# Products with B kept in their PSUM bank and scanned from there, in the two scan attentions of a four-layer adaLN network, with the order of all engines' steps laid out anew

## The chip, the cores and the metric

One Trainium2 chip, one of its cores. The time is the device time in microseconds of one launch of the whole program; the profile is of one further execution of the same program on the same core.

## The reference, cut to what matters

Four layers, each an attention-like block and a feed-forward block with adaLN modulation, on x of 4 x 512 x 128 values (2,048 rows of 128). Two of the attention-like blocks hold a recurrence along the sequence of 2,048 rows. The text calls them by the kernel's names: L2A is the retention block with index 2 ("the second" of the change's words), L3A the selective state-space block with index 3 ("the third").

```
# L2A (retention), per head of 8 channels: a decaying state of outer products of k and v
scores[i, j] = (q_i . k_j) * decay ** (i - j)   for j <= i
out          = group_norm(scores @ v) @ WO
# L3A (state space), 128 channels D, 16 states N
dt = softplus(x @ Wdt + bdt);  A = -exp(A_log)
h[t] = exp(dt[t] * A[:, n]) * h[t-1] + dt[t] * x[t] * B[t, n]      # for each n of 16
y[t] = sum over n of C[t, n] * h[t][:, n];  out = (y * silu(z)) @ Wout
```

The kernel lays channels on the 128 partitions and rows of the sequence along the free dimension. So L3A's recurrence is, for each n, one scan over 512 columns of h = A*h + B*dx, with dx = dt*x, and L2A's is, for each of 8 columns n of v, one scan of s = decay*s + k*v.

## The kernel before, in words

**Strands.** The 2,048 rows are cut into four chunks of W = 512. Each chunk c (0 to 3) runs through all eight blocks (L0A, L0F, L1A, L1F, L2A, L2F, L3A, L3F) as a strand; a fifth strand is the preparation. For each engine and block there is a generator (`l3a_tensor`, `l3a_vector`, ...) whose `yield`s cut it into steps. A string of letters, ORDER (4,524 letters before), says whose step is laid down next: a to e are TensorE's steps of strands 0 to 4, f to j ScalarE's, k to o VectorE's, p to t GpSimd's, u to y SyncE's. So each engine's instruction queue is a fixed merge of its strands, and an instruction that waits holds up all behind it, those of other strands too.

**Banks.** PSUM's eight banks are given out in the same order: `banks.take(s, q, name, step)` takes the bank whose last user lets go first, makes TensorE wait for that, and notes `step` as what will free it.

**L3A.** For each n of 16 TensorE spreads row n of B and of C over all partitions into a bank each (`B%d`, `C%d`, L1928 and L1931: a one-hot column times a bf16 split of B and C in three parts). ScalarE makes A = exp(dt*A_n) into one of four buffers AH (L1976). For even n VectorE multiplies the bank by dx into a buffer of the three in BH (L2027) and scans it in place (L2035). For odd n ScalarE copies the bank into that buffer (L1985), GpSimd multiplies it there by dx (L2059), and VectorE scans it (L2035). Then VectorE multiplies the C bank by the scanned state into A's buffer (L2039), ScalarE keeps the state's last column for the next chunk (`carry3`, L1989), GpSimd adds A's buffers of each two n (`sum`, L2065), and TensorE adds the sum to bank Y with an identity matmul (L1939). A scan of chunk c > 0 begins with chunk c-1's last column.

**L2A.** TensorE makes column n of v in all places (L1592), for even n VectorE multiplies the bank by k into a buffer of four, KV (L1663), for odd n ScalarE copies the bank (L1623) and GpSimd multiplies it by k (L1715). VectorE scans each in place with a decay that is one value to a partition (L1671), ScalarE keeps the last column (L1627), GpSimd multiplies by q (L1721), and TensorE sums over the key's eight channels into bank R (L1597).

**Around them.** While strands 0 and 1 are in L3A (about 625 to 770 us) the others' L0F, L2A and L2F run beside them; while 2 and 3 are in L3A (about 970 to 1,112 us) L2F of strand 3 and L3F of strands 0 and 1 do, whose weights come by indirect DMA from GpSimd's queue (L2459) and whose rows go out and back through SyncE's and GpSimd's (L2511, L2517, L2462, L2442).

## Time and profile before

| | us |
|---|---|
| median of 3 runs | 1228.77 |
| lowest, highest | 1224.02, 1233.12 |
| the profiled execution | 1225.84 |
| its span in the trace | 1223.8 |

In the profile a row of engine busy time counts instructions from start to end; two that follow each other at once overlap a little. "Idle before, releaser" is the time that the engine stood still ahead of the instruction and what ended it. PE is TensorE's matmul side, PEld its weight loads, DVE VectorE, ACT ScalarE, POOL GpSimd. PEclk is the granted TensorE clock as a share of the full one. The chain is the work that ended last, followed back from the last instruction.

### The profile page before, as it was taken

What the parts mean: (1) busy time and instruction counts of PE and PEld (TensorE: products, weight loads), DVE (VectorE), ACT (ScalarE), POOL (GpSimd) and SP (SyncE); (2) the same over time, 40 slices, a digit from 0 to 9 for tenths busy, and PEclk for the clock granted to TensorE, in tenths of its full rate; (3) what the DMA queues carried; (4) which work ended last, traced back from release to release, by engine and by line L of the source; (5) the groups of instructions that cost most, each with busy time, mean ns of one, the idle gap of its engine ahead of it and who ended that gap; (6) DMA issues with size and microseconds to landing.
All of it is one profiled execution on the core that took longest, in us unless ns stands there. A gap on an engine that the chain in (4) does not pass through costs nothing.

```text
span 1223.8 us, 18281 instructions
## 1 busy us (share of the span) xinstructions
PE 1082.9 (88%) x6855; PEld 654.4 (53%) x6855; DVE 872.7 (71%) x2050; ACT 685.5 (56%) x1155; POOL 493.8 (40%) x475
## 2 busy tenths in 40 slices
PE   7999999899999899999999867779899987659978
PEld 5766544344444354456444313464568676338868
DVE  4745547567666768788799899675686989966446
ACT  4477566686745586655676724562525786544221
POOL 2014122212213520184246456525455465686363
PEclk9999999999999789999999868769799998869989
DMA  8103000000000000000000000000514043147583
GB/s 257 57 9 138 1 1 0 1 1 2 1 1 18 1 2 1 20 1 1 18 1 1 0 0 1 1 3 33 172 52 166 33 164 112 33 168 232 209 291 92
DMA packets 36071, 70.14 MB, mean 57 GB/s; under 512 B 3088, under 2 KB 26128, under 8 KB 35472
## 3 DMA queue, kind: packets, MB, share of 16 engines
q0 software_dynamic: 9680, 45.88, 10.6%
q1 hardware_dynamic: 26304, 23.10, 6.0%
q8 instruction: 54, 0.88, 0.3%
q14 instruction: 33, 0.27, 0.1%
HBM read 59.34 MB, written 9.63 MB: 56 GB/s over the span
## 4 chain that ended last, share of the span: by engine, by line
PE 60%; DVE 14%; POOL 8%; ACT 8%; issue 6%; DMA 2%; another core or an unknown queue 1%; DVEq 0%; SPq 0%; POOLq 0%; ACTq 0%
PE ps L899 9%; PE ps L2177 5%; PE ps L1477 5%; PE ps L2185 3%; DVE own L2035 2%; PE ps L861 2%; PE ps L673 2%; PE ps L1276 2%; PE ps L1751 1%; PE ps L659 1%; POOL own L2059 1%; POOL own L1721 1%; PE ps L1455 1%; PE ps L1754 1%
## 5 line engine op out<-in xcount | busy, mean ns | idle before, releaser
L899 PE MATMUL ps<-own,g_f 128*128 128x512 f32 x320 | 147.8, 602 | 0.1
L899 PEld LDWEIGHTS ps<-own,g_f 128*128 128x128 f32 x320 | 59.2, 191 | 67.2 <-issue 61.0
L1226 POOL TENSOR_TENSOR own<-own 128x512 f32<-128x512 f32 x32 | 40.1, 1254 | 131.1 <-PE ps L899 95.5
L2035 DVE TENSOR_TENSOR_SCAN own<-own,carry 128x512 f32<-128x512 f32 x48 | 77.7, 1618 | 15.5 <-POOL own L2059 13.6
L2059 POOL TENSOR_TENSOR own<-own 128x512 f32<-128x512 f32 x32 | 50.7, 1585 | 53.2 <-ACT own L1985 53.0
L1939 PE MATMUL ps<-own,g_c 128*128 128x512 f32 x64 | 44.5, 784 | 30.5 <-POOL own L2065 30.4
L1976 ACT ACTIVATE own<-own,Acol 128x512 f32<-128x512 f32 x64 | 45.2, 714 | 40.1 <-PE ps L1939 38.9
L1895 POOL TENSOR_TENSOR own<-own 128x512 f32<-128x512 f32 x32 | 44.5, 1392 | 55.7 <-DVE own L1869 35.9
L1477 PE MATMUL ps<-g_l,own 128*128 128x512 f32 x128 | 59.5, 611 | 7.7 <-issue 7.3
L531 ACT ACTIVATE own<-xs,sm 128x128 f32<-128x128 f32 x128 | 52.5, 483 | 24.0 <-POOL sm L523 24.0
L2399 DVE TENSOR_TENSOR own<-ps,own 128x512 f32<-128x512 f32 x53 | 36.1, 682 | 41.4 <-PE ps L2177 13.3
L2257 ACT ACTIVATE own<-ps 128x512 f32<-128x512 f32 x53 | 31.2, 596 | 60.1 <-PE ps L2177 49.4
L514 POOL TENSOR_SCALAR sm<-sm 128x4 f32<-128x4 f32 x32 | 9.5, 299 | 135.6 <-DVE sm L506 134.8
L1721 POOL TENSOR_TENSOR own<-own 128x512 f32<-128x512 f32 x32 | 45.0, 1408 | 37.5 <-ACT carry L1627 37.5
L1396 DVE SCALAR_TENSOR_TENSOR own<-ps,own 128x512 f32<-128x512 f32 x64 | 43.0, 683 | 21.6 <-ACT own L1365 21.4
L1362 ACT ACTIVATE own<-ps 128x512 f32<-128x512 f32 x64 | 37.5, 587 | 31.1 <-PE ps L1276 30.4
L1108 DVE TENSOR_TENSOR own<-own 128x512 f32<-128x512 f32 x32 | 27.9, 871 | 36.9 <-PE ps L899 35.1
L2177 PE MATMUL ps<-own,early 128*128 128x128 f32 x384 | 50.2, 281 | 1.4 <-issue 1.4
L2177 PEld LDWEIGHTS ps<-own,early 128*128 128x128 f32 x384 | 48.2, 197 | 4.9 <-issue 4.4
L2177 PE MATMUL ps<-own,g_f 128*128 128x128 f32 x336 | 45.1, 285 | 5.6 <-DVE own L1733 2.3
L1671 DVE TENSOR_TENSOR_SCAN own<-decay_sb,carry,own 128x512 f32<-128x512 f32 x24 | 43.5, 1815 | 6.0 <-POOL own L1715 5.8
L1597 PEld LDWEIGHTS ps<-g_c,own 128*128 128x128 f32 x256 | 33.6, 202 | 26.3 <-POOL own L1721 23.3
(498 smaller groups left out, 2984.7 us busy)
## 6 DMA issues: line engine op xcount, KB each, us to landing
so<-own SPq DMA_DIRECT2D x10, 256.0 KB
g_l<-p_l SPq DMA_DIRECT2D x1, 2449.0 KB, 13.4
own<-sx SPq DMA_DIRECT2D x9, 256.0 KB, 9.5
g_f<-p_f SPq DMA_DIRECT2D x1, 2223.5 KB, 10.6
own<-cs SPq DMA_DIRECT2D x8, 256.0 KB, 3.4
sx<-brow SPq DMA_DIRECT2D x2, 960.0 KB, 12.4
g_l<-p_l SPq DMA_DIRECT2D x1, 1866.0 KB, 7.9
sx<-brow SPq DMA_DIRECT2D x1, 1472.0 KB, 14.3
```

Source lines behind the costliest of these rows:

```text
L531: m = e.activation(tl(T[c][0], i), xs[:, 4 * c + i, :], ACT.Identity, bias=nm[:, i:i + 1], scale=rs[:, i:i + 1])
L899: x = e.matmul(s.bank["V%d%d%d" % (it, k, cc)][:, :], ew2[:, m, 128 * cc:128 * cc + 128], gm, start=False, stop=m == 3)
L1396: e.scalar_tensor_tensor(out=E, in0=s.bank["m%d%d" % (hd, k)][:, :], scalar=1.0, in1=E, op0=ALU.add, op1=ALU.max).then_inc(*s.dve.up("m%d% ...
L1477: m = e.matmul(p[:, :], tl(T[c][6 + k], i), w21[:, k, 512 * half:512 * half + 512], start=k == 0, stop=k == 1)
L1671: e.tensor_tensor_scan(kv, decay.broadcast_to([128, W]), kv, init, ALU.mult, ALU.add).then_inc(*s.dve.up("scan%d" % n))
L1721: e.tensor_tensor(st, st, T[c][6], ALU.mult).then_inc(*s.pool.up("q%d" % (n - 1)))
L1895: e.tensor_tensor(g, T[c][FU[m % 3]], T[c][FT[m % 2]], ALU.mult).then_inc(*s.pool.up("m%d" % m))
L1939: e.matmul(s.bank["Y"][:, :], V["ident"], T[c][AH[(2 * k) % 4]], start=k == 0, stop=k == 7).then_inc(*s.pe.up("Y%d" % k))
L1976: e.activation(T[c][AH[n % 4]], dt, ACT.Exp, scale=Acol[:, n:n + 1]).then_inc(*s.act.up("A%d" % n))
L2035: e.tensor_tensor_scan(H, A, H, init, ALU.mult, ALU.add).then_inc(*s.dve.up("H%d" % n))
L2059: e.tensor_tensor(b, b, T[c][6], ALU.mult).then_inc(*s.pool.up("B%d" % n))
L2177: m = e.matmul(tl(p, f), tl(w, f), x, start=True, stop=True)
```

## The change

1. L3A, odd n (8 in each strand, 32 in all): ScalarE's copy and GpSimd's product are gone; VectorE makes the product, as for even n.
2. L3A, all n (64): VectorE's product is written back into the bank of B itself, and the scan reads the bank and writes the buffer BH. The bank's freeing step is the scan (H), no longer the product or the copy. The waits for BH's earlier users stand ahead of the scan, no longer ahead of the product.
3. L2A, even n (16 in all): the same, the bank's freeing step is the scan; odd n are left as they are.
4. ORDER is laid out anew: 4,492 letters (32 fewer of ScalarE, 32 fewer of GpSimd, 32 more of VectorE). Read as merges, the two strings let the strands' blocks overlap in the same way in every queue. Among TensorE's 1,448 steps one that signals stands on average 3 places from where it stood, at most 34; strand 0's L3A runs over places 740 to 923 there where it ran over 738 to 908, strand 2's over 1,107 to 1,254 where it ran over 1,102 to 1,258.

```diff
@@ l2a_tensor
-                    p = banks.take(s, q, "v%d" % n, (s.act if n % 2 else s.dve, "v%d" % n))
+                    p = banks.take(s, q, "v%d" % n, (s.act, "v%d" % n) if n % 2 else (s.dve, "scan%d" % n))
@@ l2a_vector
                     if n % 2:
                         yield
                         q.wait_ge(*s.pool("kv%d" % n))
+                        fresh = kv
                     else:
                         yield
                         q.wait_ge(*s.dve("qT"))
+                        q.wait_ge(*s.pe("v%d" % n))
+                        fresh = s.bank["v%d" % n][:, :]
+                        e.tensor_tensor(fresh, fresh, T[c][4], ALU.mult).then_inc(*s.dve.up("v%d" % n))
+                        yield
+                        q.wait_ge(*s.dve.now())
                         if n >= 4:
                             q.wait_ge(*s.pe("R%d" % (n - 4)))
-                        q.wait_ge(*s.pe("v%d" % n))
-                        e.tensor_tensor(kv, s.bank["v%d" % n][:, :], T[c][4], ALU.mult).then_inc(*s.dve.up("v%d" % n))
-                        yield
-                        q.wait_ge(*s.dve.now())
@@
-                    e.tensor_tensor_scan(kv, decay.broadcast_to([128, W]), kv, init, ALU.mult, ALU.add).then_inc(*s.dve.up("scan%d" % n))
+                    e.tensor_tensor_scan(kv, decay.broadcast_to([128, W]), fresh, init, ALU.mult, ALU.add).then_inc(*s.dve.up("scan%d" % n))
@@ l3a_tensor
-                    p = banks.take(s, q, "B%d" % n, (s.act if n % 2 else s.dve, "B%d" % n))
+                    p = banks.take(s, q, "B%d" % n, (s.dve, "H%d" % n))
@@ l3a_scalar
-                    if n % 2:
-                        yield
-                        q.wait_ge(*s.pe("B%d" % n))
-                        if n == 1:
-                            q.wait_ge(*s.dve("part32"))
-                        if n >= 3:
-                            q.wait_ge(*s.dve("C%d" % (n - 3)))
-                            q.wait_ge(*s.act("c%d" % (n - 3)))
-                        e.activation(T[c][BH[n % 3]], s.bank["B%d" % n][:, :], ACT.Copy).then_inc(*s.act.up("B%d" % n))
@@ l3a_vector
-                    if n % 2:
-                        yield
-                        q.wait_ge(*s.pool("B%d" % n))
-                    else:
-                        yield
-                        q.wait_ge(*s.pe("B%d" % n))
-                        if n >= 3:
-                            q.wait_ge(*s.act("c%d" % (n - 3)))
-                            q.wait_ge(*s.dve("C%d" % (n - 3)))
-                        e.tensor_tensor(H, s.bank["B%d" % n][:, :], dx, ALU.mult).then_inc(*s.dve.up("B%d" % n))
-                        yield
-                        q.wait_ge(*s.dve.now())
+                    fresh = s.bank["B%d" % n][:, :]
+                    yield
+                    q.wait_ge(*s.pe("B%d" % n))
+                    e.tensor_tensor(fresh, fresh, dx, ALU.mult).then_inc(*s.dve.up("B%d" % n))
+                    yield
+                    q.wait_ge(*s.dve.now())
+                    if n >= 3:
+                        q.wait_ge(*s.act("c%d" % (n - 3)))
+                        q.wait_ge(*s.dve("C%d" % (n - 3)))
                     q.wait_ge(*s.act("A%d" % n))
@@
-                    e.tensor_tensor_scan(H, A, H, init, ALU.mult, ALU.add).then_inc(*s.dve.up("H%d" % n))
+                    e.tensor_tensor_scan(H, A, fresh, init, ALU.mult, ALU.add).then_inc(*s.dve.up("H%d" % n))
@@ l3a_gpsimd
-                if n < 16 and n % 2:
-                    b = T[c][BH[n % 3]]
-                    yield
-                    q.wait_ge(*s.act("B%d" % n))
-                    q.wait_ge(*s.dve("dx"))
-                    e.tensor_tensor(b, b, T[c][6], ALU.mult).then_inc(*s.pool.up("B%d" % n))
@@ ORDER: 38 lines of letters out, 38 in
```

## Rows read from the trace of the kernel before

**Rows 1.** The page: busy time of each engine, and the chain's shares by engine.

```profile
PE 1082.9 (88%) x6855; PEld 654.4 (53%) x6855; DVE 872.7 (71%) x2050; ACT 685.5 (56%) x1155; POOL 493.8 (40%) x475
...
PE 60%; DVE 14%; POOL 8%; ACT 8%; issue 6%; DMA 2%; another core or an unknown queue 1%; DVEq 0%; SPq 0%; POOLq 0%; ACTq 0%
```

**Rows 2.** Windows: each engine's busy time by stretch, granted clock, DMA share.

```profile
core 0: us, PE busy (x) PEld busy (x) DVE busy (x) ACT busy (x) POOL busy (x), PEclk, DMA share, GB/s
...
390.00:625.00 235.00, 221.17 (x1818) 119.26 (x1817) 188.73 (x481) 151.47 (x253) 84.17 (x81) 0.94 0.02 6
625.00:770.00 145.00, 114.26 (x331) 47.63 (x329) 135.80 (x171) 80.20 (x144) 82.91 (x57) 0.85 0.00 1
770.00:950.00 180.00, 157.15 (x1292) 108.49 (x1291) 120.86 (x352) 81.56 (x154) 81.78 (x87) 0.87 0.22 74
950.00:1112.00 162.00, 123.45 (x726) 88.91 (x725) 138.91 (x224) 98.47 (x162) 104.86 (x89) 0.88 0.32 107
```

**Rows 3.** Groups by line and shape, whole span: the work touched by the change.

```profile
L2059 POOL TENSOR_TENSOR own<-own 128x512 f32<-128x512 f32 x32 | 50.7, 1585 | 53.2 <-ACT own L1985 53.0
...
L1671 DVE TENSOR_TENSOR_SCAN own<-decay_sb,carry,own 128x512 f32<-128x512 f32 x24 | 43.5, 1815 | 6.0 <-POOL own L1715 5.8
...
L1859 DVE TENSOR_SCALAR own<-ps,g_l 128x512 f32<-128x512 f32 x32 | 23.6, 737 | 6.8 <-PE ps L1764 6.6
...
L1985 ACT ACTIVATE own<-ps 128x512 f32<-128x512 f32 x32 | 18.6, 582 | 9.9 <-PE ps L1928 9.9
...
L1671 DVE TENSOR_TENSOR_SCAN own<-decay_sb,own 128x512 f32<-128x512 f32 x8 | 12.7, 1591 | 0.0
```

**Rows 4.** One line's instructions: duration in ns as min/median/max, first and last start.

```profile
L2035 DVE TENSOR_TENSOR_SCAN own<-own,carry x48: 1264/1283/3064, 695.7 to 1104.2; 128x512 f32<-128x512 f32 x48
...
L1671 DVE TENSOR_TENSOR_SCAN own<-decay_sb,own x8: 1193/1251/2286, 391.7 to 419.6; 128x512 f32<-128x512 f32 x8
...
L2039 DVE TENSOR_TENSOR own<-ps,own x64: 648/680/693, 632.3 to 1106.5; 128x512 f32<-128x512 f32 x64
...
L1108 DVE TENSOR_TENSOR own<-own x32: 656/692/1747, 106.7 to 674.6; 128x512 f32<-128x512 f32 x32
```

**Rows 5.** Timeline near 1,035 us: start, duration, engine, line, operation.

```profile
1034.83 1.26 POOL L2065 TENSOR_TENSOR own<-own 128x512 f32<-128x512 f32 x1
1034.90 2.28 DVE L2035 TENSOR_TENSOR_SCAN own<-own,carry 128x512 f32<-128x512 f32 x1 [1.10 <-POOL own L2059]
...
1036.05 2.19 POOL L2059 TENSOR_TENSOR own<-own 128x512 f32<-128x512 f32 x1
...
1037.28 1.27 DVE L2039 TENSOR_TENSOR own<-ps,own 128x512 f32<-128x512 f32 x2
```

**Rows 6.** Groups in 625 to 770 us, VectorE: L3A's scans, both shapes.

```profile
L2035 DVE TENSOR_TENSOR_SCAN own<-own,carry 128x512 f32<-128x512 f32 x16 | 25.5, 1596 | 0.6 <-POOL own L2059 0.4
L2035 DVE TENSOR_TENSOR_SCAN own<-own 128x512 f32<-128x512 f32 x16 | 24.7, 1546 | 2.6 <-ACT carry L1989 2.1 <-POOL own L2059 0.4
```

**Rows 7.** Groups in 950 to 1,112 us, VectorE: L3A's scans.

```profile
L2035 DVE TENSOR_TENSOR_SCAN own<-own,carry 128x512 f32<-128x512 f32 x32 | 52.1, 1630 | 14.9 <-POOL own L2059 13.2 <-ACT carry L1989 1.6
```

**Rows 8.** The chain's shares by line in 625:770, then in 950:1112.

```profile
by line: issue 16.7%; DVE own L2035 13.8%; PE ps L899 8.4%; DVE own L2039 6.7%; PE ps L1939 4.7%; POOL own L2059 4.3%; DVE own L2027 3.4%; POOL own L2065 2.6%; PE ps L1931 1.9%; PE ps L1764 1.8%; PE ps L1751 1.8%; PE ps L1928 1.8%; PE ps L1
...
by line: issue 11.9%; PE ps L2177 11.1%; POOL own L2059 7.0%; DVE own L2035 6.3%; POOL sx L2462 5.8%; PE ps L2185 4.7%; DMA g_f<-w,slot 4.5%; POOL own L2065 4.4%; DMA g_f<-w,where 3.5%; PE ps L1939 3.2%; DVE own L1863 2.6%; DVE own L1733 2.
```

**Rows 9.** Waits, whole span: who waited for whom, total, times, longest.

```profile
PEld ps L1939 <- POOL own L2065: 31.2, 14, 10.1
PE ps L1939 <- POOL own L2065: 30.4, 13, 9.6
...
PEld ps L1931 <- DVE own L2039: 19.3, 11, 4.4
...
DVE own L2035 <- POOL own L2059: 14.0, 11, 3.0
...
PE ps L1931 <- DVE own L2039: 10.3, 8, 3.1
```

More of the change, by code:

```diff
@@ new lines @@
+    "kbdfgllrrbbaagkrrheakbdfkkkdkbdndkglyaanlnfanjdgnffbfaainninafdgnajddnfiakfkabfakbfkbgnakbkckhakaapaddkfdlikdkfdinnaatga"
+    "qkeddllipdddlqaaqininnqqagddfkddnddiaaafaaifdpdnnnnnafkkbdgkkpiaakpfdiaiiddnfddfdofnndnndonfkdiddkidkddkidkidkdnanaiianf"
+    "dddafnkaafaifidkdkdkdnaaaaaafffaiiffdaffkkdaapnaiasoaaaaaannpffftbbbqfnsbqagggsbbbgssibbkaallllllgfkkkkggkgkpabbbkaaglll"
+    "llbbffaaaaffgggbbgkpaggllaalblllpafkkkbkblbblfkbbglfdlilgbbbgbbbfflgqbkgpfbqkbkblkbkbqgkbbbgkgbklgkbbllqafllaabqgffafaag"
@@ new lines @@
+    "gakkgkafakrkrgcccchlkpllpchhhpccplfcmlclhhbhbhabgccfgaglamfmmahmmfbkfmmmbbpmgmkaafgffbfkflfccflflacfbbbhkfhhchbhlkkfbbhk"
+    "bmqmgmgbgglgccgccmbbhmcgchcmhafcmamamammkffkkfacccfkfcrcckffkfckhfmaaaarccffffhkfackkkfkffamaccaccchrfkfkkfchmhkfaacchmr"
+    "ffmcmfmfahfkfkkbfafakkbrkkfkaabbbhakabhbbggghkaalkkhkgmqbbbmlmmqbmmlmkccglkalgbbblfballcbgkkbgqkppblhgcppfbbqhbhlahccfah"
+    "glllllckkakmgakggkkamaffkamcccgkfkmqkckkfllcclhlhclhlcfkfallkkkkhbbkamkbgagbfafbbgkbkkaalghhlcclcgrbbclccclalrckqccqkkkq"
@@ L72 @@
+    "mchmdmcsccmcrhnncnmccmrncnicnnndhrmccwunchnnncnnccnmcmcccnmrhnssmnmcnhncndssnccnidmdmihnsddwidicncndnidmmidddidncnndndis"
+    "sdddiimwdnrnndindddrrsidridnnndndrssidddidinxxsnndddidindrndsddndindissrnrddndxindsddndnnidsdddndnxindiddndnnddddidnnndd"
+    "idddmndmndiddnmdnmdidnmdddnssssssdidssnndndnwdnnnnnx"
 )
```

65 lines of the change are left out of this document (27 added, 38 removed).

## The prediction

> **What bounds the kernel now.** I read the page first. TensorE's matmul side is busy 88% of the span and holds 60% of the chain, VectorE is busy 71% and holds 14%, GpSimd 8% with 40% busy [rows 1]. That average hides stages, so the second view is the windows by stage [rows 2]. From 390 to 625 us TensorE is busy 221 of 235 us: there it is the limit. In the two stretches that hold L3A it is not: 114 of 145 us in 625 to 770, 123 of 162 us in 950 to 1,112, with the granted clock at 0.85 and 0.88, against 0.94 before. VectorE is busy 136 of 145 us in the first and 139 of 162 us in the second. So the first stretch is VectorE's, and the second belongs to no engine alone: there dependencies set the pace, and the lines of the chain tell which [rows 8]. TensorE's idle time in the two is 31 + 39 = 70 us; that is the ground on which a change to L3A can win.
>
> The third view is single durations. A scan from SBUF takes 1,283 ns in the median and up to 3,064 [rows 4], and its mean is 1,596 and 1,546 in the first stretch and 1,630 in the second [rows 6, 7]. The product of bank and SBUF tensor (L2039), just as often and in the same stretches, is never over 693 ns, while a product of two SBUF tensors (L1108) is 692 in the median and up to 1,747 [rows 4]. The timeline shows what stretches them: at 1,034.83 GpSimd begins a sum of two SBUF tensors, 70 ns later VectorE begins a scan, and the scan takes 2.28 us; GpSimd's next product begins at 1,036.05 under that scan and takes 2.19 us [rows 5]. Each holds up the other for the length of one operation. VectorE's operations with one input in PSUM are not held up.
>
> **What the change does to VectorE's load.** It adds 32 products. Two products back to back take 1.27 us [rows 5], the first by itself 0.68 [rows 4], so one more costs 0.60 us of the queue: 32 x 0.60 = +19.2 us, half in each stretch. All 64 products of L3A and 16 of L2A now write to PSUM, which no row shows VectorE doing. Bounds: 0.68 us as for the nearest product, and 0.74 us as for the dearest operation on a bank (L1859 [rows 3]), which would add 80 x 0.06 = 5 us. I take the first; L2039 and L1108 differ by 12 ns in the median, so where the operand lies has cost next to nothing.
>
> It takes the contention from all L3A scans if the reading above is right, since they will have A in SBUF and the product in PSUM. First stretch: 25.5 + 24.7 - 32 x 1.28 = 9.2 us [rows 4, 6]. Second: 52.1 - 41.0 = 11.1 us [rows 4, 7]. Together -20.3 us. A scan from PSUM has no row either: its lower bound is the median 1.25 us of the scans without carry [rows 4], its upper the present mean of about 1.6, which is no gain at all. I take 1.28, because the products stand at that end. L2A's 32 scans take 43.5 + 12.7 = 56.2 us [rows 3], 1.76 each, against 1.25 undisturbed [rows 4]: 16 of them freed give 16 x 0.51 = -8.1 us. Odd scans of L2A keep both inputs in SBUF. GpSimd's 32 products (50.7 us) go [rows 3]; they held up other two-SBUF operations too, which I put at -3 us over both stretches, from L1108's spread. ScalarE loses 32 copies, 18.6 us [rows 3]; its work in neither stretch is near the limit (80 of 145, 98 of 162 [rows 2]), so this counts for nothing by load. If ScalarE were full, the copies would be worth their 18.6.
>
> The Trainium skill says why it could be so: its page SBUF — State Buffer, section Who interferes with whom, has a VectorE instruction with two SBUF inputs contend with a GpSimd instruction that reads SBUF, and one with at most one SBUF input not. By that rule, the trace agrees: L2039's 693 ns against L1108's 1,747. Another page speaks against the change: Perfetto Trace Analysis, section Optimizing Scalar/DVE Operations, gives VectorE about 60 ns of overhead on SBUF and about 125 on PSUM. By it 80 scans would pay 65 ns each, an estimate of 5 us that takes back part of the gain.
>
> **What of it lies on the path.** First stretch: VectorE is the limit there, so its load counts: +9.6 - 9.2 - 1.5 (half of the 3) - 1.0 (the few L2A scans there) = -2 us, and its idle time ahead of scans is 3 us [rows 6], of which I take 1. I count -3. So the contention's relief is here almost all spent on the products that moved. Second stretch: GpSimd's product is on the chain, 7.0% of 162 = 11.3 us [rows 8], and VectorE stands idle for it 13.2 us of its 14.9 [rows 7]. In its place stand products of 0.60 us: 11.3 us of the chain at 1.585 us each [rows 3] are 7 pieces, +4 us. The scans' pieces are 6.3% = 10.2 us, of which a fifth is contention (1,630 against 1,283 ns), -2. That makes -9, and since VectorE is then the next limit (139 of 162 us before) I count -8. The L2A scans in 390 to 625 and 770 to 950: 8.1 - 1.0 = 7 us less of VectorE, but that is under TensorE's limit in the former (221 of 235). Half of what is left lies on the path at best; I count -3. Sum: -3 - 8 - 3 = -14 us.
>
> What becomes late next: in the first stretch VectorE itself. In the second, GpSimd's sums and its weights' DMAs, and TensorE's matmul behind the sum, for which its matmul side stands idle 30.4 us (the 31.2 on its loads' side are largely other sights of the same gaps) [rows 9]. The sums' queue on GpSimd is now free of products, so they start at once after the C product; I leave that uncounted; it is the bigger rival's (3).
>
> Moved steps: the wait for the buffer's earlier users (Y, carry, C product three n before) moves from the product to the scan. That lets the product run earlier; its work is the same and the queue behind it the same, price nothing while a step of another strand stands between product and scan; if none does, the scan waits for what the product waited for before, which is again nothing. No DMA is issued by a removed step. GpSimd's indirect DMAs stand behind 32 instructions less. SyncE's queue is passed by none of the code's edits; only ORDER shifts its steps' neighbours.
>
> **ORDER.** It moves TensorE's steps by 3 places on average and lets the same blocks overlap. Outside the two stretches TensorE is idle 141 - 70 = 71 us of 917 in all. A merge laid out for other costs can win or lose some of it; a tenth, +-7 us, is what I allow, and none in the sum.
>
> The profiled execution is 1225.84 us, 2.93 below the median of the runs shown. 1225.8 - 14 = 1211.8; with the median's distance 1214.7, which I round to 1214.
>
> **Rivals.** (1) *The bank is held too long, slower.* A B bank was freed by a product or a copy, now by the scan behind it, 1.28 us later at least, and later still if A's exp or the chunk before it is late, as all behind the scan's wait on VectorE is then. TensorE's loads already wait 19.3 us and its matmuls 10.3 us for the C product to free a bank, 19 times [rows 9]; those are banks running short. If one hold in three of the 64 comes out as TensorE's wait of a scan and a half, that is 21 x 1.9 = +40 us less the 14: about +26, 1252 by the median; if one in five, +10, about 1239. It decides from some 8 of the 64 on (8 x 1.9 = 15 us, all the gain). Against it: TensorE is ahead of VectorE in the first stretch by so much that waiting costs nothing while VectorE is full. The PSUM — Partial Sum Buffer page of the Trainium skill, in its summary of rules, says to evacuate promptly; by that rule the change goes the wrong way, and no row here gives it a price.
>
> (2) *No relief.* A scan with one input in the bank is stretched as before, or the sums and L2A's products collide instead. Then VectorE has +19.2 us and gets back only the idle 14.0 us before scans [rows 9]: first stretch +9, second -8, near 1230.
>
> (3) *Everything on the chain comes back.* Sums earlier too: half of the 30.4 us that TensorE's matmuls wait for them [rows 9] is 15 us more. With less idle time its clock in the two stretches could also be nearer to the 0.94 of the stretch before them [rows 2]. About 1198.
>
> (4) *The gain is given back later*, in L3F's DMAs and TensorE's own load, or by ORDER: 1226.
>
> **Chances.** Forecast (its own range 1203 to 1222) 0.42; (3) 0.14; (4) 0.13; (2) 0.12; (1) 0.19. About 1% is what a measurement of this kernel can tell from no change, since three runs of it span 0.7%. Faster by over 1% is below 1216.5: 0.35 of the forecast's, all of (3), 0.01 of (4): 0.50. Slower by over 1% is above 1241: 0.14 of (1) and 0.02 of (2), with 0.01 of (4), 0.17. Within 1%: 0.33. The range leaves out the far half of (1) and of (3): 1195 to 1242.
>
> **What would show it.** Right: L2035's mean near 1,280 ns and its longest below 1,500; VectorE's busy time down by some 10 us though it has 32 instructions more; L2059 gone, GpSimd near 440 us or below; TensorE's waits for L2065 down in the second stretch; the first stretch no shorter than by 3 us. Wrong: scans above 1,500 ns in the mean (rival 2), TensorE's waits at L1928 and L1931 put down to L2035 (rival 1), or a window outside the two stretches that has changed by over 7 us (ORDER).

## The result and the profile after

The changed kernel takes 1239.05 us in the median of 20 runs (1232.27 to 1244.49), the kernel before 1229.74 us in the median of 20 runs beside them. The ratio is 1.0071, with an interval of 1.0055 to 1.0087: slower by 9 us, where 14 us less were forecast. The profiled execution took 1243.94 us (span 1241.9), 4.9 above its median, while the one before (1225.84) lay 3.9 below the median of the 20; so the two traces differ by 18.1 us where the medians differ by 9.3.

The page of the kernel after: the span, the engines' busy time, the chain by engine. The lines answer to [rows 1].

```profile
span 1241.9 us, 18213 instructions
...
PE 1085.7 (87%) x6855; PEld 662.1 (53%) x6855; DVE 857.2 (69%) x2082; ACT 679.9 (55%) x1130; POOL 421.4 (34%) x443
...
PE 26%; DVE 9%; ACT 4%; issue 4%; POOL 3%; DMA 2%; another core or an unknown queue 1%; SPq 0%; DVEq 0%; POOLq 0%
```

VectorE is busy 15.5 us less with 32 instructions more, and GpSimd 72 us less. The engines' load fell as it was meant to, and the kernel became slower. (The chain of this trace covers only about half of the span, so its shares by engine aren't compared with those of before.)

The windows by stage after, to be read against [rows 2]:

```profile
core 0: us, PE busy (x) PEld busy (x) DVE busy (x) ACT busy (x) POOL busy (x), PEclk, DMA share, GB/s
390.00:625.00 235.00, 217.19 (x1787) 119.41 (x1785) 178.27 (x466) 144.04 (x240) 75.03 (x77) 0.91 0.02 6
625.00:770.00 145.00, 113.43 (x336) 49.38 (x337) 129.69 (x177) 82.80 (x137) 44.18 (x37) 0.88 0.00 1
770.00:950.00 180.00, 159.24 (x1304) 111.04 (x1303) 130.82 (x369) 80.26 (x159) 88.32 (x95) 0.86 0.20 65
950.00:1112.00 162.00, 124.80 (x690) 86.56 (x690) 132.81 (x247) 95.48 (x153) 72.91 (x73) 0.87 0.32 106
```

VectorE is busy 6 us less in each L3A stretch. The same clock times of two runs don't hold the same work, though, so the place of the loss has to be read from fixed points of the computation. Good ones are the additions that end a strand's block, x += output. The strand with the number 1 is the second of the four, strand 3 the last. Here is VectorE's timeline (start, duration) in the kernel before: the end of strand 1's L2F, strand 1's L3A, strand 3's L2F, strand 3's L3A, and the last block.

```profile
661.48 0.67 DVE L1885 TENSOR_TENSOR xs<-ps,xs 128x512 f32<-128x512 f32 x1
...
796.48 0.68 DVE L2046 TENSOR_TENSOR xs<-ps,xs 128x512 f32<-128x512 f32 x1
...
980.57 0.66 DVE L1885 TENSOR_TENSOR xs<-ps,xs 128x512 f32<-128x512 f32 x1
...
1114.77 0.69 DVE L2046 TENSOR_TENSOR xs<-ps,xs 128x512 f32<-128x512 f32 x1 [1.31 <-issue]
...
1220.41 0.69 DVE L2428 TENSOR_TENSOR xs<-ps,xs 128x512 f32<-128x512 f32 x1 [0.52 <-PE ps L2155]
```

The same five in the kernel after (L1887, L2036 and L2412 are the same additions):

```profile
667.13 0.69 DVE L1887 TENSOR_TENSOR xs<-ps,xs 128x512 f32<-128x512 f32 x1 [0.47 <-PE ps L1766]
...
798.48 0.67 DVE L2036 TENSOR_TENSOR xs<-ps,xs 128x512 f32<-128x512 f32 x1
...
994.33 0.69 DVE L1887 TENSOR_TENSOR xs<-ps,xs 128x512 f32<-128x512 f32 x1
...
1120.07 0.69 DVE L2036 TENSOR_TENSOR xs<-ps,xs 128x512 f32<-128x512 f32 x1 [0.34 <-PE ps L1948]
...
1238.47 0.69 DVE L2412 TENSOR_TENSOR xs<-ps,xs 128x512 f32<-128x512 f32 x1 [0.52 <-PE ps L2139]
```

Subtracting the ends of neighbours (start plus duration) gives the time of each piece. The last three columns are the same points in runs told below: a_oldorder and a_again are one kernel on two chips, the changed instructions in the order of before; f_again, on a_again's chip, has the new order around the first L3A stretch alone. All are single executions.

| piece, us | before | after | a_oldorder | a_again | f_again |
|---|---|---|---|---|---|
| start to end of strand 1's L2F | 662.1 | 667.8 | 656.0 | 659.8 | 661.2 |
| to end of strand 1's L3A | 135.0 | 131.3 | 141.6 | 140.4 | 127.5 |
| to end of strand 3's L2F | 184.1 | 195.9 | 187.1 | 187.2 | 182.0 |
| to end of strand 3's L3A | 134.2 | 125.7 | 130.5 | 130.6 | 132.6 |
| to the end | 105.6 | 118.4 | 104.9 | 107.9 | 107.6 |

The two pieces with L3A at their end did become shorter, by 3.7 and 8.5 us. The three others became longer by 5.7, 11.8 and 12.8: 30 us lost against 12 won. The prediction worked out the two and allowed the three +-7 together. The description of the change has the strands' blocks overlap in the same way in both orders. Between these points that isn't quite so: strand 0's own L3A ends at 774.6 in the kernel after and at 744.8 in the kernel before. In the new order the two L3As of the first stretch end 25 us apart, in the old one 52.

A last view looks into the first piece. At 450.91 the kernel before begins the addition that ends strand 1's L1A (L1435), the kernel after at 465.83: 15 us behind before the new instructions of L3A exist, with only the first of L2A's run. Not all of it is lost time, since the new order also shifts work between strands: by the end of strand 1's L2F the lag is 5.7. Windows of 6 us show TensorE's granted clock just ahead, before:

```profile
406.00:412.00 6.00, 5.51 (x100) 2.83 (x104) 4.89 (x7) 2.46 (x7) 2.11 (x3) 0.72 0.01 3
412.00:418.00 6.00, 4.78 (x49) 3.11 (x36) 5.93 (x8) 3.80 (x6) 3.96 (x3) 0.67 0.00 0
418.00:424.00 6.00, 5.32 (x6) 1.35 (x6) 4.16 (x6) 1.36 (x2) 0.00 (x0) 0.50 0.01 3
424.00:430.00 6.00, 6.00 (x31) 3.04 (x30) 1.36 (x2) 3.95 (x7) 2.48 (x2) 0.97 0.00 0
430.00:436.00 6.00, 5.37 (x143) 3.21 (x142) 5.93 (x13) 5.84 (x12) 0.00 (x0) 0.88 0.01 3
```

and after:

```profile
406.00:412.00 6.00, 3.35 (x13) 1.69 (x12) 5.22 (x4) 4.22 (x10) 3.98 (x4) 0.86 0.00 0
412.00:418.00 6.00, 6.00 (x45) 3.41 (x44) 4.74 (x6) 3.17 (x6) 2.32 (x3) 0.50 0.01 3
418.00:424.00 6.00, 6.00 (x49) 4.06 (x47) 3.50 (x6) 2.91 (x6) 0.82 (x1) 0.50 0.00 0
424.00:430.00 6.00, 6.00 (x93) 4.32 (x97) 2.70 (x5) 3.01 (x8) 2.94 (x2) 0.50 0.01 3
430.00:436.00 6.00, 5.21 (x100) 2.47 (x101) 5.41 (x9) 4.24 (x7) 0.00 (x0) 0.50 0.01 3
```

TensorE stands idle for 2.65 us in 406 to 412, and then runs 24 us at half clock (1.2 GHz), where before it had 6. Over 400 to 460 the granted clock is 0.72 against 0.83, over 460 to 530 it is 0.95 against 0.98. The share of the clock withheld times the length is 16.8 + 3.5 = 20.3 us in the one and 10.2 + 1.4 = 11.6 in the other. (That is a measure of the dip, not of time lost: where TensorE isn't what all wait for, a slow clock costs less.)

### The profile page after: what moved, and what is told of

It reads as the page before. It is cut to its first block and busy times, and to the rows that moved or that the text cites. A ratio compares the mean times of both kernels' runs of the same rounds, so it can differ in the third digit from the quotient of the medians.

```text
span 1241.9 us, 18213 instructions
## 1 busy us (share of the span) xinstructions
PE 1085.7 (87%) x6855; PEld 662.1 (53%) x6855; DVE 857.2 (69%) x2082; ACT 679.9 (55%) x1130; POOL 421.4 (34%) x443
## 5 line engine op out<-in xcount | busy, mean ns | idle before, releaser
L1226 POOL TENSOR_TENSOR own<-own 128x512 f32<-128x512 f32 x32 | 40.7, 1272 | 172.3 <-PE ps L899 105.2
L899 PEld LDWEIGHTS ps<-own,g_f 128*128 128x128 f32 x320 | 59.1, 190 | 71.2 <-issue 63.3
L2025 DVE TENSOR_TENSOR_SCAN own<-own,carry,ps 128x512 f32<-128x512 f32 x48 | 61.1, 1274 | 5.3 <-ACT own L1978 3.7
L2049 POOL TENSOR_TENSOR own<-own 128x512 f32<-128x512 f32 x32 | 41.7, 1308 | 67.7 <-DVE own L2029 67.5
L1897 POOL TENSOR_TENSOR own<-own 128x512 f32<-128x512 f32 x32 | 43.4, 1356 | 47.0 <-DVE own L1871 23.9
L1941 PE MATMUL ps<-own,g_c 128*128 128x512 f32 x64 | 42.6, 753 | 17.8 <-POOL own L2049 12.9
L1723 POOL TENSOR_TENSOR own<-own 128x512 f32<-128x512 f32 x32 | 44.1, 1385 | 27.4 <-ACT carry L1627 27.4
L2161 PE MATMUL ps<-own,early 128*128 128x128 f32 x384 | 48.7, 276 | 2.1 <-DMA early<-w,where 0.9
L2161 PEld LDWEIGHTS ps<-own,early 128*128 128x128 f32 x384 | 46.4, 192 | 5.7 <-issue 3.5
L1597 PEld LDWEIGHTS ps<-g_c,own 128*128 128x128 f32 x256 | 36.9, 213 | 21.7 <-issue 11.4
L2161 PE MATMUL ps<-own,g_f 128*128 128x128 f32 x336 | 45.2, 288 | 1.8 <-DMA g_f<-w,slot 1.8
L2161 PEld LDWEIGHTS ps<-own,g_f 128*128 128x128 f32 x336 | 43.4, 204 | 5.6 <-issue 2.9
L2014 DVE TENSOR_TENSOR ps<-ps,own 128x512 f32<-128x512 f32 x64 | 43.9, 688 | 3.4 <-PE ps L1930 3.3
## 6 DMA issues: line engine op xcount, KB each, us to landing
own<-sx SPq DMA_DIRECT2D x9, 256.0 KB, 11.8
g_f<-p_f SPq DMA_DIRECT2D x1, 2223.5 KB, 10.3
sx<-brow SPq DMA_DIRECT2D x1, 1472.0 KB, 10.3
```

Source lines behind the costliest of these rows:

```text
L899: x = e.matmul(s.bank["V%d%d%d" % (it, k, cc)][:, :], ew2[:, m, 128 * cc:128 * cc + 128], gm, start=False, stop=m == 3)
L1723: e.tensor_tensor(st, st, T[c][6], ALU.mult).then_inc(*s.pool.up("q%d" % (n - 1)))
L1897: e.tensor_tensor(g, T[c][FU[m % 3]], T[c][FT[m % 2]], ALU.mult).then_inc(*s.pool.up("m%d" % m))
L1941: e.matmul(s.bank["Y"][:, :], V["ident"], T[c][AH[(2 * k) % 4]], start=k == 0, stop=k == 7).then_inc(*s.pe.up("Y%d" % k))
L2014: e.tensor_tensor(fresh, fresh, dx, ALU.mult).then_inc(*s.dve.up("B%d" % n))
L2025: e.tensor_tensor_scan(H, A, fresh, init, ALU.mult, ALU.add).then_inc(*s.dve.up("H%d" % n))
```

## The experiments

No kernel here leaves work out. Ratios are to the kernel before on the same chip, with a 95% interval. The chips differ (before's median is 1216.9 on one and 1230.4 on another), so ratios are compared, and microseconds only within one chip. A difference of two such ratios is uncertain by some 0.3%, that is 3 to 4 us, or more. Two theories stood at first: the instructions make the loss (banks held too long, rival 1), or the order does.

**Instructions alone, order alone.** a_oldorder has the changed instructions in the letters of before; a few of TensorE's steps, whose bank now comes free only with a scan, stand a few letters later, and in TensorE's own queue two neighbours have changed places. b_neworder has the instructions of before in the letters of after, with GpSimd's product put just ahead of its scan; o_neworder_early has them with GpSimd's product as early as its copy allows.

```diff
 a_oldorder:       instructions of after
-ORDER of after
+ORDER of before, 32 letters of ScalarE and GpSimd out, VectorE's products in
 b_neworder, o_neworder_early:  instructions of before
-ORDER of before
+ORDER of after, ScalarE's copies and GpSimd's products put in (late; early)
```

> The changed instructions with the order of before: its steps keep their places, the removed ones are left out, the new product of odd n stands just ahead of its scan, and a TensorE step whose bank would not yet be free is put off by the few places that this takes. Theory 1 (the new order is what costs): 1215 to 1222, 8 to 14 below the kernel before, with the same stage times as before up to the first scan of L2A. Theory 2 (the longer hold of the banks costs, the order is neutral or helps): 1238 or more.

> The changed instructions with the order of before throughout, once more and on the same chip as the run before. If the new order's worth in L3A's first stretch is 13 us: ratio 0.997 to 1.001, 12 to 18 us above the run before, and the second chunk's L3A ends 133 to 143 us after its L2F against 124 to 129.

> The instructions of before with the order of the changed kernel: ScalarE's copy right behind A's exp, GpSimd's product at the place of the new product. Theory 1: slower than the kernel before by 15 or more, 1245 to 1255, and some 10 to 15 of it there by the end of the third chunk's L1A (about 527 before). Theory 2: 1225 to 1233, no slower than before.

> The instructions of before with the new order once more, this time with GpSimd's product as early as its input allows and not just ahead of the scan (the earlier run of this kind came out at 1.0844). If that result came from the late place of GpSimd's product: 1.005 to 1.03. If the new order does not fit the old instructions wherever the product stands (TensorE's C and B steps are merged for a scan that follows at once): 1.05 or more.

a_oldorder: 0.9988 (0.9964 to 1.0013), and on another chip, as a_again, 1.0004 (0.9977 to 1.0032). So the instructions alone change nothing that these runs can tell, and the order of after costs 1.0071 - 0.9988 = 0.8%, 10 us (0.7% by a_again). b_neworder: 1.0844 (1.0801 to 1.0887); o_neworder_early: 1.0768 (1.0732 to 1.0804). The new order doesn't suit the old instructions: the waits of b_neworder in 625 to 850 us (who for whom: us in total, times, longest) are those of its product's path, which no longer fits its places.

```profile
POOL own L2059 <- ACT own L1985: 60.2, 10, 9.7
...
PE ps L1939 <- POOL own L2065: 41.0, 10, 7.2
...
DVE own L2035 <- POOL own L2059: 22.3, 11, 4.1
```

Putting the product early (o_neworder_early) cured hardly a tenth of it. "Instructions" and "order" are not two costs to be added: the same order costs 0.8% with the one set of instructions and 8% with the other.

**Which part of the order.** With the changed instructions, the letters of before and after can be joined at a step that both have in hand. What was joined:

```
c_oldfirst     before's order up to the first product of L2A (about 350 us), then after's
d_newfirst     after's up to there, then before's
e_oldtail      after's up to the end of strand 2's L3A (about 1,045 us), then before's
f_oldnewold    before's up to the end of strand 1's L2F (about 656 us),
               after's up to the end of strand 1's L3A, then before's
j_newfrom450   as f, but after's order from the end of strand 1's L1A (about 450 us) on
k_oldclock     after's order, but before's from the first product of L2A
               to the end of strand 1's L1A
```

> The changed instructions; the order of before up to the first product of L2A (some 1,440 steps, none of them changed), the new order from there. Theory 1 with its loss ahead of L2A: 1224 to 1230, 10 to 15 below the changed kernel. If the loss is behind L2A's beginning, or is not the order's: 1236 to 1242.

> The changed instructions; the new order up to the first product of L2A, the order of before from there. Theory 1 with its loss ahead of L2A: 1228 to 1235, that is about 12 over the changed instructions in the order of before. If the first part of the order is neutral: equal to the changed instructions in the order of before within 3.

> The changed kernel with the new order up to the end of the third chunk's L3A (about 1,050 us) and the order of before from there. Theory tail (GpSimd's gathers of earlier chunks' rows stand ahead of the last chunk's weight fetches in the new order, and TensorE stands still for them near 1,180): 1229 to 1233, 7 to 9 below the changed kernel, and no idle time of over 8 us at L2124. Rival (the second part of the new order loses its 8 us between L2A and L3A, and the tail only passes it on): 1237 to 1240.

> The changed instructions; the order of before up to the second chunk's L2F end (656 us there), the new order up to the second chunk's L3A end, the order of before from there. If the new order is what L3A's first stretch wants (131 us for it in the run with the old order first, 142 with the old order throughout): 1214 to 1218, below both kernels. If that gain is only the recovery of what the new order had put off before: 1224 to 1230.

> The best kernel so far once more (changed instructions; order of before up to 656 us, the new one up to the second chunk's L3A end, order of before again), beside the next run on the same chip. If its gain is its own and not the first chip's: ratio 0.982 to 0.989.

> The changed instructions; the order of before up to the end of the second chunk's L1A (449 us in the run with the order of before throughout), the new order up to the end of the second chunk's L3A, the order of before from there. If the new order is the better one from there on (201 us from that point to the second chunk's L2F end, against 207 in the order of before): ratio to the kernel before 0.978 to 0.984, below the run that took the new order from 656 us only (0.9858). If those 6 us were only the making up of an earlier delay: 0.984 to 0.990.

> The changed kernel with the order of before in one place only, from the first product of L2A (about 355 us) to the end of the second chunk's L1A (about 460). Clock theory (in the new order TensorE's clock is at half from about 410 to 436 without a break, in the order of before it comes back between, and 9 to 13 us of the changed kernel's loss arise there): ratio 0.996 to 1.001, against 1.0071, the second chunk's L1A ends at 452 to 456 in place of 466.5, and the granted clock in 400 to 460 is 0.8 or more in place of 0.7. Rival (what is lost there is made up behind it, since VectorE sets the pace from 625 on): 1.003 to 1.008.

| run | ratio | interval |
|---|---|---|
| c_oldfirst | 1.0032 | 1.0006 to 1.0059 |
| d_newfirst | 1.0022 | 0.9997 to 1.0047 |
| e_oldtail | 1.0038 | 1.0016 to 1.0059 |
| f_oldnewold | 0.9858 | 0.9833 to 0.9884 |
| f_again, another chip | 0.9887 | 0.9839 to 0.9935 |
| j_newfrom450 | 0.9975 | 0.9949 to 1.0001 |
| k_oldclock | 1.0027 | 1.0002 to 1.0051 |

The first 350 us of the new order cost 0.34% (d less a) or 0.39% (after less c); the rest costs 0.44% (c less a) or 0.49% (after less d). By the ratios each difference is hardly larger than its uncertainty. But a, c and d ran on one chip: there d's median is 5.4 us above a's, and every run of c (1230.59 and more) is slower than every run of a (1229.76 and less), by 8.1 us in the median. So both parts cost something; how much each is known only roughly, 0.8 or 1.1% together by the one count and the other. In the first part the trace shows no more than that TensorE is busy 105.1 us of the first 120 against 109.5. Within the rest the tail behind strand 2's L3A costs 0.33% by the ratios (after less e, on two chips; more on that below). The stretch around the first L3A, 656 to 800 us, is the opposite of a cost: f is 1.3% faster than a, and on one chip f_again takes 14.5 us less than a_again (1216.63 and 1231.11). Adding after's order from 450 to 656 us to f (j) costs 1.2%, 14 us (0.9% against f_again), and most of it is paid later, since from the end of strand 1's L2F to that of its L3A j takes 137.9 us. But j is no slower than a (0.9975 and 0.9988): the gain around L3A and this cost cancel, so a piece of an order has no price of its own apart from what stands before and behind it.

**What the pieces of the other traces add.** Three pieces of the first table can be compared in all these kernels, one execution each, all with the changed instructions:

| piece, us | before's order there | after's order there |
|---|---|---|
| end of strand 1's L3A to end of strand 3's L2F | 174.4 to 187.2 (a, a_again, d, f, f_again, j) | 192.8 to 196.5 (after, c, e, k, p) |
| to end of strand 3's L3A | 130.5 to 132.6 (the same) | 123.4 to 125.7 (the same) |
| to the end, chips of e, f, j, k | 101.4 to 102.0 (e, f, j) | 100.8 (k) |
| to the end, the other chips | 104.9 to 107.9 (a, a_again, d, f_again) | 114.1 to 118.4 (after, c, p) |

(e has after's order only up to the middle of the second of these pieces.) So the new order delays strand 3's L2F on every chip, by 12 us in the kernel after, and the shorter L3A behind it wins back only part. Of the 8.5 us won in the second L3A stretch the 5 to 7 that come with the new order may be no more than this shift. No run exchanges the order in that piece alone. And the tail of the new order costs 7 to 13 us on some chips and nothing to be seen on k's. That weakens each comparison across these two groups of chips: after less e and after less k may hold the chip's part too.

**The clock.** The clock withheld over 400 to 530 us, summed as above, is 8.4 us in a_oldorder, 11.6 in before and d_newfirst, 13.8 in f_oldnewold, 18.6 in j, 20.3 in after, c_oldfirst and e_oldtail. k_oldclock puts before's order where the clock falls in after, up to 450 us. Its ratio is 0.44% lower than after's, about half of the order's 0.83%, but its chip is one on which the new tail costs nothing to be seen. In its trace the dip moved and kept its size: 0.77 in 400 to 460 and 0.88 in 460 to 530 are 22.2 us withheld, and strand 1's L1A ends at 460.6, against 466.5 in after, 462.5 in c_oldfirst and 448.9 in a_oldorder. That trace isn't typical, though: the execution took 1231.79 us at a mean granted clock of 0.912, where the median is 1223.44 and five of the twelve took 1216 to 1218 us at 0.927 to 0.931. What the dip is in those no trace shows, so this run doesn't decide the clock theory.

Two things speak against a clock that simply follows the order. a_again and f_again have the same instructions and the same letters up to 656 us and ran on one chip; still a_again has 0.86 in 400 to 460 us and f_again 0.77, and their twins on other chips the same two values, so 5.4 us of withheld clock come and go with the order unchanged. And over the whole span after and a_oldorder have the same granted clock in the median of their runs, 0.92, at 0.8% difference in time. What remains is this: the kernels with after's order in 460 to 530 us (after, c, e, j, k) have 10 to 14 us more withheld over 400 to 530 than a_oldorder, those with before's order there (before, d, f) 3 to 5. Whether the clock falls for the idle time that the order makes, or the order loses time by itself as well, these runs don't separate.

**The tail.** GpSimd lays out the gathers of rows (L2426) and the fetches of weights (L2443) of L3F. In after's order six gathers stand among four fetches near 1,180 us, five of them ahead of three of the fetches. p_gathers puts all four fetches first.

```diff
 GpSimd's order near 1,180 us, p_gathers
-gather x3, g_f, gather x2, g_f, g_l x2, gather
+g_f x2, g_l x2, gather x6
```

> The changed kernel with six letters of its order exchanged, all GpSimd's near 1,177 to 1,190 us: four weight fetches of the last chunk stand ahead of the six gathers of another chunk's rows, not among them. TensorE's, VectorE's, ScalarE's and SyncE's queues are the same. Tail theory (the fetches come 5 to 6 issues of 1.25 us late, and TensorE stands still for their weights): 1.002 to 1.005 against 1.0071, that is 3 to 6 us, and TensorE's stand at L2124 near 1,180 us shrinks from 12.4 to below 8. If the gathers are what is waited for, or the weights' transfer itself is the limit: 1.006 to 1.010.

1.0077 (1.0047 to 1.0107), as after. In the timeline TensorE's largest stand of the tail, in front of L2124, was this one in after:

```profile
1192.32 2.04 PE L2124 MATMUL ps<-own 128*128 128x128 f32 x8 [12.40 <-issue]
```

and in p_gathers:

```profile
1180.10 2.05 PE L2124 MATMUL ps<-own 128*128 128x128 f32 x8 [5.75 <-issue]
...
1191.35 2.04 PE L2124 MATMUL ps<-own 128*128 128x128 f32 x8 [5.02 <-DVE own L2329]
```

One stand of 12.4 us became two of 10.8 together, and the tail takes 116.2 us instead of 118.4. The theory that these fetches hold up the tail falls. What in the tail's order costs the 7 to 13 us of some chips stays open.

**Which instructions.** Three kernels in the letters of before (with the few places that their banks need), one part at a time, and two in orders joined as f's:

```diff
 g_l2a_only:   L2A's even products in the bank; L3A as before
 l_evenonly:   the same, and of L3A the even products only; odd n stay ScalarE's copy and GpSimd's product
-    p = banks.take(s, q, "B%d" % n, (s.act if n % 2 else s.dve, "B%d" % n))
+    p = banks.take(s, q, "B%d" % n, (s.act, "B%d" % n) if n % 2 else (s.dve, "H%d" % n))
 h_sbuf:       as a_oldorder, but L3A's products go to BH, and the bank is free at the product
-    p = banks.take(s, q, "B%d" % n, (s.dve, "H%d" % n))
+    p = banks.take(s, q, "B%d" % n, (s.dve, "B%d" % n))
-    e.tensor_tensor(fresh, fresh, dx, ALU.mult)
+    e.tensor_tensor(H, fresh, dx, ALU.mult)
-    e.tensor_tensor_scan(H, A, fresh, init, ALU.mult, ALU.add)
+    e.tensor_tensor_scan(H, A, H, init, ALU.mult, ALU.add)
 m_sbuf_f:     h_sbuf's instructions in f_oldnewold's order
 n_best:       l_evenonly's instructions in an order joined as f_oldnewold's
```

> The kernel before with L2A's even products made and scanned in their bank, L3A and the order as before. Relief theory: 1221 to 1225, 3 to 7 below the kernel before, from L2A's scans near 1.28 us instead of 1.76, and with it L3A's part of the change costs 1 to 5 (the run with both parts in the order of before is 1225.8). If L2A's part is worth nothing: 1227 to 1229.

> The order of before, L2A's part, and of L3A only this: the even products stay in their bank and are scanned there, the odd ones stay with ScalarE and GpSimd. No product is moved to VectorE, half of the scans are relieved. Load theory (L3A's part costs 4 us in the order of before since VectorE has 32 products more in the stretch where it is full): below L2A's part alone, ratio 0.989 to 0.995. Hold theory (the longer hold of the B banks costs TensorE more than the relief brings): above it, 0.997 to 1.002.

> The order of before and both parts, but L3A's products are all VectorE's from bank to the SBUF buffer, so that a bank is let go of at the product, and the scan reads two SBUF tensors. If the longer hold of the banks is what costs L3A its gain: below 1225.8, 1217 to 1223, and the first L3A stretch is shorter than 142 us. If the relief from GpSimd is worth more than the hold: 1228 to 1240, with L3A's scans at 1.4 us or more.

> The order that ran at 0.9858 (before's up to 656 us, the new one up to the second chunk's L3A end, before's again), but L3A's products, all VectorE's, are written to the SBUF buffer and scanned there: GpSimd's contention is back, the hold of the banks is short. If the scan from the bank is worth something where VectorE is full: 0.989 to 0.994. If relief and hold cancel here as they did in the order of before (0.9988 and 0.9986): 0.984 to 0.988.

> The two best findings together: L2A's part and L3A's even products kept in their bank, L3A's odd n as in the kernel before, with the order of before up to 656 us and from the second chunk's L3A end on, and the new order between (ScalarE's copy behind A's exp, GpSimd's product behind the copy). If relief without load and the new order for that stretch add up: ratio 0.976 to 0.984, below both 0.9858 and 0.9901. If the new order's gain there rests on all products being VectorE's: 0.990 to 1.01, since GpSimd's two-microsecond detour then stands in a queue laid out without it.

| run | ratio | interval |
|---|---|---|
| g_l2a_only | 0.9954 | 0.9927 to 0.9981 |
| l_evenonly | 0.9901 | 0.9874 to 0.9929 |
| h_sbuf | 0.9986 | 0.9965 to 1.0007 |
| m_sbuf_f | 0.9928 | 0.9903 to 0.9954 |
| n_best | 1.0100 | 1.0060 to 1.0139 |

L2A's part is worth 0.46%, 5.6 us. L3A's even products in their banks are worth 0.53% more (l less g), 6.5 us. Moving the odd ones to VectorE as well takes 0.9% away again (a less l), 10.6 us, in this order. These runs are on different chips, but the traces place this loss where chips hardly differ: strand 1's L3A ends at 788.4 us in l_evenonly and at 797.6 in a_oldorder. The VectorE groups of l_evenonly show that one mechanism at work on both sides of one line: L2039 is its scan, from SBUF for odd n, from the bank for even n.

```profile
L2039 DVE TENSOR_TENSOR_SCAN own<-own,carry 128x512 f32<-128x512 f32 x24 | 42.9, 1786 | 9.8 <-POOL own L2063 9.5
...
L2039 DVE TENSOR_TENSOR_SCAN own<-own,carry,ps 128x512 f32<-128x512 f32 x24 | 30.6, 1274 | 2.3 <-ACT carry L1991 2.2
```

h_sbuf has its products on VectorE but scans from SBUF:

```profile
L2025 DVE TENSOR_TENSOR_SCAN own<-own,carry 128x512 f32<-128x512 f32 x48 | 72.8, 1518 | 4.8 <-ACT carry L1982 3.7
...
L2025 DVE TENSOR_TENSOR_SCAN own<-own 128x512 f32<-128x512 f32 x16 | 23.1, 1445 | 3.3 <-ACT carry L1982 2.9
```

Its scans take 95.9 us where a_oldorder's take 80.8, 15 us more on VectorE, and still 0.9986 stands beside 0.9988. So in before's order the longer hold of the bank seems to cost what the relief brings, within some 3 us: h_sbuf exchanges the two together, and no run has the one without the other. In f's order m_sbuf_f (0.9928) is 0.7% behind f_oldnewold and 0.4% behind f_again: there the relief is worth something net of the hold (of the two distances only the first is clear of noise).

**Why a_oldorder loses where f_oldnewold wins.** From the end of strand 1's L2F to the end of its L3A before takes 135.0 us, a_oldorder 141.6 and a_again 140.4, f_oldnewold and f_again 127.5, the last four with the same instructions. 656 to 800 us in a_oldorder (TensorE's two sides, VectorE, ScalarE, GpSimd, clock):

```profile
656.00:800.00 144.00, 107.12 (x469) 47.10 (x471) 115.12 (x186) 65.60 (x129) 44.06 (x42) 0.76 0.00 1
```

and in f_oldnewold:

```profile
656.00:800.00 144.00, 113.69 (x728) 53.64 (x730) 128.72 (x209) 73.04 (x144) 47.59 (x47) 0.81 0.00 1
```

VectorE, nearly full in before (126 of 144), is idle 29 us in a and 15 in f. TensorE's longest waits in a in 640 to 800 us are for banks:

```profile
PE ps L1933 <- DVE own L2025: 8.4, 5, 2.4
PE ps L1930 <- DVE own L2025: 6.4, 5, 2.1
```

The matmuls that spread B and C wait 14.8 us for a bank that a scan holds. But f_oldnewold has the same two rows with 6.3 and 5.7 us, 12.0 in 9 waits, so these waits alone don't part the slow order from the fast one. VectorE's idle time tells them apart better. In a_oldorder, 640 to 800 us, it begins with

```profile
DVE own L2025 <- ACT carry L1982: 6.8, 4, 2.9
DVE own L1108 <- PE ps L899: 6.2, 2, 4.1
DVE own L1644 <- PE ps L1585: 3.3, 3, 1.6
```

(the scan waits for the carried column, other strands' work for TensorE), where f_oldnewold has no wait of a scan for the carry and 2.1 us of the second. VectorE's products of L3A wait 0.8 us in a_oldorder. Every engine stands a little for the next: short waits with nobody full, and the granted clock is lower too, 0.76 against 0.81. That the new order around L3A takes the loss away is shown by the f and a pairs on two chips; which of the letters does it, and how much of it is the clock, was not tried.

**The best version.** f_oldnewold beats both kernels: 1202.69 us against 1216.94 for before on its chip, 1216.63 against 1230.44 on another. l_evenonly, 1204.63 against 1218.20 (0.9901), can't be told from the second of these (0.9887), with hardly an edit to the order. Joining the two (n_best) gave 1.0100. f's order is made for odd products on VectorE; in n_best they take the way over ScalarE and GpSimd, whose product waits 47.7 us for the copy in 656 to 812 us, against 32.9 in before.

## Why the prediction was wrong, step by step

**Which stretches are bound by what: right where it was read, too narrow where it was used.** That L3A's stretches had the idle time to win was borne out: TensorE's matmuls wait for GpSimd's sums 12.9 us in all after, against 30.4 [rows 9], and the two pieces with L3A became 3.7 and 8.5 us shorter.

**The relief of the scans: right.** VectorE's instructions of the scan's line after (ns, min/median/max):

```profile
L2025 DVE TENSOR_TENSOR_SCAN own<-own,carry,ps x48: 1247/1278/1281, 723.3 to 1102.0; 128x512 f32<-128x512 f32 x48
L2025 DVE TENSOR_TENSOR_SCAN own<-own,ps x16: 1207/1220/1221, 642.6 to 749.9; 128x512 f32<-128x512 f32 x16
```

The longest of 64 is 1,281 ns, against 3,064 in [rows 4], with GpSimd's sums beside them. L3A's scans take 80.6 us against 102.3 [rows 6, 7]: 21.7 less, where 20.3 were forecast. L2A's take 47.5 against 56.2 [rows 3]: 8.7 less, forecast 8.1. The half of them left in SBUF still shows the contention, side by side in the groups of after:

```profile
L2014 DVE TENSOR_TENSOR ps<-ps,own 128x512 f32<-128x512 f32 x64 | 43.9, 688 | 3.4 <-PE ps L1930 3.3
...
L1673 DVE TENSOR_TENSOR_SCAN own<-decay_sb,carry,own 128x512 f32<-128x512 f32 x12 | 20.4, 1703 | 3.9 <-POOL own L1717 3.9
...
L1673 DVE TENSOR_TENSOR_SCAN own<-decay_sb,carry,ps 128x512 f32<-128x512 f32 x12 | 15.3, 1277 | 0.3
```

The product that writes its bank (L2014) takes 688 ns, at the lower bound taken (0.68). Rival (2), no relief, is out. By the Trainium skill's page SBUF — State Buffer, Who interferes with whom, a VectorE instruction with at most one input in SBUF, outside its 2-port modes, doesn't contend with GpSimd: the trace agrees, for scans too. Its page Perfetto Trace Analysis, Optimizing Scalar/DVE Operations, would have made scans from PSUM dearer; the durations here don't show that (1,278 against 1,283 ns), and the measurement decides.

**L2A: right in direction, sized too small.** Forecast -3 us, measured -5.6 alone (g_l2a_only). The sum counted less than half of its 8 us, since TensorE was busy 221 of 235 us there. That busy time is not a limit at every moment is the likely reason; no run shows it.

**First L3A stretch: -3 forecast, +6.6 in the order of before.** This is the first step that failed. The sum netted loads of VectorE, which was nearly full in before, and took it that it would stay full. It did not: of the 144 us VectorE is busy 11 less than before, and the piece is longer. Part of the 6.6 isn't L3A's: g_l2a_only, with L3A as before, takes 138.7 us for the piece, 3.7 more than before. The rest comes with the odd products: l_evenonly, where they stay off VectorE, takes 131.9. The wait that rival (1) names is real: after has TensorE's matmuls wait 16.6 us in 14 waits for the scans of L3A where before had 10.3 in 8 for the C product [rows 9], and a_oldorder 14.8 us in 10 of them in that stretch alone. But a wait is 1.2 to 1.5 us, against 1.9 assumed, f_oldnewold has 9 of the same in that stretch and is fast, and h_sbuf, with the short hold, is no faster than a_oldorder: at most the hold takes back the relief, and the +26 of the rival never showed. (Its 1252 was counted from the profiled execution; from the median, as the text there says, it is 1255.)

**Second L3A stretch: -8 forecast, -3.8 in the order of before, -8.5 in the new one, part of which may be the shift told above.** GpSimd's product left the chain, and VectorE's products came in its place. In a_oldorder the chain's shares by line in 950 to 1,112 us begin with issue 11.7%, DVE L2025 11.5%, PE L2161 8.5%, DMA own<-sx 7.9% and DVE L2014 6.8%: the scan's and the product's share, 18.3% of 162 us, is 30 us, where scan and GpSimd's product had 13.3% [rows 8]. The step "7 pieces of 0.60, +4 us" was too small: an engine that was busy 139 of 162 us took in 16 products, and stayed at 139.28.

**ORDER: 0 +- 7 us forecast, +10 us measured (0.83%), and not one thing.** This is the second step that failed, and the one that turned nothing won into a loss. "A tenth of TensorE's idle time outside the stretches" had no ground in what an order does. Its pieces are of both signs and some larger than their sum: +0.34 to 0.39% in the first 350 us, +1.2% for 450 to 656 us (j less f), -1.3% around the first L3A (f less a), some 12 us up to the end of strand 3's L2F and 7 to 13 in the tail of some chips, by the traces. "3 places on average" says nothing of time. The prediction named the sign to look for, a window outside the two stretches changed by over 7 us, and there are two. Rival (4) had the order give the gain back, but stopped at zero.

**The range and the clock.** 1239 lies inside 1195 to 1242, close to its end. The clock entered only with rival (3), as something to be gained in L3A's stretches; the stretch where it moved, 400 to 460 us, was not looked at, though the kernel before shows 0.50 in 418 to 424 there. How much of the 9 us the clock makes stays open.

## What to carry to other kernels

When a change comes with a new global order, price the two apart, and don't price an order at nothing because its steps moved by few places: here its pieces were worth as much as the whole change, up and down. Measure the changed instructions in the old order, and the new order by stretches; here the kernel to ship was a third one, the new order for one stretch only, 1.1 to 1.4% faster than before. 15 us less work on an engine that is nearly full came out as nothing here (h_sbuf against a_oldorder), probably since the same edit makes it hold a buffer longer. And compare orders on one chip, and on traces of typical executions: the tail's cost here depended on the chip, and one trace lay 8 us above its median.

## What the runs showed of the hardware that was not expected

TensorE's granted clock was 0.50 in four windows of 6 us in a row, 412 to 436 us, in the kernel after, with its matmul side busy 23.2 of the 24 us; the engine had stood idle 2.65 us in the 6 us ahead, and the work was mostly L1A's and L2A's matmuls, about half of the time in ones of 16 to 32 columns. In the kernel before one window in that stretch was at 0.50. In the same stretch two kernels with the same instructions and letters so far differ on one chip: 406 to 412 us is at 1.00 in a_again and at 0.77 in f_again.

A scan that reads its data from a bank and writes SBUF, 512 columns, is steady to 3% (1,247 to 1,281 ns in 48), and a product that reads and writes the same bank costs no more than one that only reads it: 688 against 684 ns (L2014, L2029).

The same kernel differs by chip: before had medians of 1216.94, 1218.20, 1228.02, 1229.58 and 1230.44 us on five chips, more than most of the differences studied. Where chips differ is seen in f_oldnewold and f_again, one kernel: 661.5 and 661.2 us up to the end of strand 1's L2F, 127.5 and 127.5 for the next piece, 132.3 and 132.6 for the fourth, but 174.4 and 182.0 for the third and 102.0 and 107.6 for the last. The 13 us between the two executions lie in these two pieces. Both run beside DMA (f_again's share is 0.26 in 800 to 950 us and 0.58 behind 1,112), but so does the fourth (0.37), and what makes the difference isn't shown.
